# A four-layer decoder on one core: the expert layer on all eight experts, or on the two chosen per token through rows sorted in DRAM

## The chip, the cores and the metric

The kernel runs on one core of one Trainium2 chip. The metric is the device time of one execution in microseconds. The engines are PE (matmul), DVE and ACT (elementwise), POOL (GpSimd) and SP, which here only issues transfers.

## The reference, cut to what matters

x is 4 batches of 1024 tokens of 256 features, float32. Four residual layers follow one another: an attention both ways with a context of 77 rows, an expert layer, a one-head attention to the context, and an MLP with ternary weights. The expert layer is what the change touches:

```python
probs = softmax(layernorm(x) @ Wr)             # 8 experts
topk_p, topk_i = top_k(probs, 2)
# for each of the token's two experts e:  y_e = (xn @ Wi[e]) @ Wo[e]
x = x + tanh(g_ffn[0]) * sum_k(topk_p[k] * y_{topk_i[k]})
```

## The kernel before, in words

Every engine has its own program, written out by hand in the order of its work, and the programs meet at semaphores; there is no planner. An engine runs its list strictly in order. x stays in SBUF as 32 tiles of 128 tokens (x_residual), eight tiles a batch (JT), four tiles a group (G), eight groups (NG).

Stage A is the first attention, one batch after another (c = 1 to 3 in all engines' lists, batch c's scores beside a_sum of batch c-1; the a_sums of batch 3 run into stage B). Per tile, a_sum is seven products on PE, a tanh on ACT (line 1024), two updates on DVE (lines 1428, 1430) and two additions to x on POOL (lines 1778, 1780). In its first part the products Wi[e] @ Wo[e] are made and kept as wexp_h and wexp_l, a high and a low part in float32r: products of two such operands are summed as high by high, high by low and low by high.

Stage B is the expert layer, all eight experts for every token. For a group: DVE normalises (normalise, line 1276), PE transposes (line 475), ACT saves the high part and DVE the low part (lines 1098, 1526), PE makes the router logits (b_route_T, line 718), DVE chooses two (b_route, lines 1539 to 1558) and forms a weight per expert, zero for those not chosen. Then b_experts runs 16 times per group: for one tile and two experts six products of 512 columns,

```python
for k in range(KC):
    for a, c in ((xTh, wexp_h), (xTh, wexp_l), (xTl, wexp_h)):
        last = mm(ps[:, 4 + i % 4, :], a[:, s, k, j * P:(j + 1) * P],
                  c[:, k, pair * 2 * D:(pair + 1) * 2 * D], ...)
```

(line 740), and DVE adds each expert's half to x with its weight (b_add, line 1571). Work of the next group is set between these steps (b_pass, in each engine's list). In the last group's pass the second attention of group 0 (c_turn to c_attend) is set between them.

Beside stage B the weights of the MLP are loaded by SP (lines 444 to 455): ACT examines them in slices of 2048 columns, 11 in all, for low bits (examine, line 1080), rounds w1, w2, h1, w3 (line 1088), and POOL rounds h2 once the experts' weights are done with (line 1797, mlp_h_rounded). A flag says whether the weights fit the short number format; PE, ACT and DVE load it into a register (line 937 on PE) and take the short branch.

Stage D is the MLP in groups, each with the second attention of the next group set between its products (group, lines 873 to 927): w1 and w2, then h1, h2 (8 output chunks of 16 products each), then w3 with 256 columns, all on line 857. POOL adds the outcome (line 1803), SP stores it. POOL's invert makes the inverse deviation of a group's normalisation (lines 1758 and 1759, a power).

Of the kernel before, what the change touches and what calls it, by code (L numbers as in the profile page):

```python
# [27 lines left out]
F32 = mybir.dt.float32  # L28
# [14 lines left out]
G = 4  # L43
# [7 lines left out]
SLICE = 2048  # L51
REST_SLICES = (NW - HC * HID) // SLICE
# [19 lines left out]
def program(nc, d):  # L72

    ctx = ExitStack()
    with ctx:
# [42 lines left out]
        mcolb = place("small", "mask_bias_of_batch", [L, 1])  # L118
# [56 lines left out]
        E1 = place("work", "probs", [P, JT, L], at=cursor["work"] - KC * BL * 4)  # L175
        ctxr = place("work", "context", [L, B, D])
# [6 lines left out]
        c2 = place("work", "score_bias_back", [L, B])  # L183
        xn = place("work", "x_normalised", [P, JT, D])
# [10 lines left out]

        wr = place("work", "router", [P, KC, E])
        wrh = place("work", "router_high", [P, KC, E], F32R)
        wrl = place("work", "router_low", [P, KC, E], F32R)
        lgT = place("work", "logits_T", [E, GN])
        c1row = place("work", "score_bias_rows", [2, BL], at=cursor["work"] - GN * 4)  # L200
        cursor["work"] += GN * 4 - 1248
        lg = place("work", "logits", [P, G, 2 * E])
        top = place("work", "top8", [P, G, E])
        want = place("work", "to_mark", [P, G, E])
        marked = place("work", "marked", [P, G, 2 * E])
        lsub = place("work", "logits_less_max", [P, G, E])
        pex = place("work", "expert_exp", [P, G, E])
        sme = place("work", "expert_sum", [P, G])
        rie = place("work", "expert_inv", [P, G])
        rig = place("work", "expert_inv_gated", [P, G])  # L210
        pm = place("work", "expert_masked", [P, G, E])
        coef = place("work", "expert_weight", [P, 2, G, E])
        assert cursor["work"] <= wk + 4 * HC * GN * 4

        xTh = place("work", "x_T_high", [P, 2, KC, GN], F32R, at=aw_at)
        assert cursor["work"] <= dead_at
        xTl = place("work", "x_T_low", [P, 2, KC, GN], F32R, at=xt_at)
        h2_part = place("work", "mlp_h2_slice", [P, SLICE], at=dead_at)
        dump = place("work", "examined", [P, SLICE], BF16)
        assert dead_at >= aw_at + KC * GN * 8  # L220
# [19 lines left out]

        xnc = place("work", "x_norm_c", [P, G, D], at=xdh_at)
# [7 lines left out]
        mcol = place("work", "mask_bias", [L, B])  # L249

# [14 lines left out]
        rest_in = sem("mlp_rest_loaded")  # L265
# [56 lines left out]
        rt_ps = sem("router_logits_T_in_psum")  # L322
        rt_s = sem("router_logits_T_saved")
        rb_ps = sem("router_logits_in_psum")
        lg_r = sem("router_exponent_ready")
        ee_r = sem("router_exp_ready")
        y_ps = sem("expert_outputs_in_psum")
        y_free = sem("expert_bank_free")
# [18 lines left out]
        rd_r = sem("weights_slice_rounded")  # L347
        part_in = sem("mlp_h2_slice_loaded")
        h2_rd = sem("mlp_h2_slice_rounded")
# [61 lines left out]
        def pair_of(i):  # L411

            return 2 * (i // E) + i % 2, i % E // 2
# [5 lines left out]
        def _(sp):  # L419
# [20 lines left out]
            sp.wait_ge(fin, NT)  # L440
            sp.wait_ge(th_r, NT)
            sp.wait_ge(xupd, NT)

            for i, examined in enumerate((0, 1, 4, 6)):
                if i:
                    sp.wait_ge(ck_r, examined)
                rows_k = SLICE // HID
                sp.dma_start(h2_part[:].rearrange("p (k c) -> p k c", k=rows_k),
                             d["h2"][:, i * rows_k:(i + 1) * rows_k, :]).then_inc(part_in, 16)
                if i == 0:  # L450
                    for n in REST:
                        sp.dma_start(mlp_f[n], d[n]).then_inc(rest_in, 16)

            sp.wait_ge(y_ps, 4 * NT)
            sp.dma_start(mlp_f["h2"], d["h2"]).then_inc(h2_in, 16)
# [13 lines left out]
        def _(pe):  # L469
# [84 lines left out]
            def a_back_scores(c):  # L554
                pe.wait_ge(xT_r, (c + 1) * JT)
                if c == 0:
                    pe.wait_ge(map_v, 5)
                else:
                    pe.wait_ge(sf_v, 2 * c)
                for h in range(2):  # L560
# [45 lines left out]
            def a_probs_T(c):  # L606
                if c < B - 1:
                    pe.wait_ge(xT_r, (c + 2) * JT)
                for q in range(2):
# [5 lines left out]
            def a_sum(b, j):  # L615
# [23 lines left out]
                mm(ps[:, second, 0:D], IT[:, t], SSl[:, b % 2, 0:D], start=False, stop=True).then_inc(fin, 1)  # L639

# [40 lines left out]
            for c in range(1, B):  # L681
# [9 lines left out]
                a_pool(c, 1)  # L691
                a_sum(c - 1, 4)
                a_sub2char(c)
                a_sum(c - 1, 5)
                if c < B - 1:
                    a_turn(c + 1, range(0, 4))
                a_sum(c - 1, 6)
                if c < B - 1:
                    a_turn(c + 1, range(4, JT))
                a_sum(c - 1, 7)  # L700
                a_probs_T(c)
# [5 lines left out]
            def b_turn(g, s, tiles):  # L707
                for j in tiles:
# [1175 lines left out]
```

## Time and profile before

| what | value |
|---|---|
| median of 3 runs | 1144.22 us (1143.49 to 1146.84) |
| the profiled execution | 1147.13 us |
| its span, first to last instruction | 1145.2 us |
| mean granted PE clock | 0.984 of full |
| PE busy | 1094.8 us (96%) |
| DVE, ACT, POOL busy | 538.0, 449.8, 120.8 us |
| chain: PE | 84%, of it line 857 52%, line 740 13% |
| stage B, first to last expert product | 171.5 to 402.0 us |
| stage D, first product | 408.3 us |

Matmuls are pipelined: a product of 512 columns is shown as some 390 ns long while the next one starts after some 230 ns. So busy times of PE are read against the spacing of starts. "Idle before" of a group is the time in which its engine waited just ahead of it, with the releaser behind the arrow.

### The profile page before, as it was taken

The page shows a single profiled execution, that of the slowest core. Times are in us where ns is not written, and L with a number is a line of the kernel's source. Part 1 is how long each engine was busy: PE and PEld are TensorE (multiplying, and loading weights), DVE is VectorE, ACT ScalarE, POOL GpSimd, SP SyncE. Part 2 cuts the span into 40 slices and gives each one's busy share as a digit, 9 for nine tenths or more (in the row PEclk, how much of TensorE's full clock was granted, in tenths as well). Part 3 has the DMA queues.
Part 4 walks back from the last instruction along what each step waited for, and adds up shares of the span by engine and source line. Part 5 has one row for each costly group of instructions (what it writes and reads, how often), then busy time and mean ns, then how long its engine had stood idle before and what let it go on. Part 6 is the DMA issues. An engine that isn't in the chain of part 4 may idle for free.

```text
span 1145.2 us, 14891 instructions
## 1 busy us (share of the span) xinstructions
PE 1094.8 (96%) x5194; PEld 865.2 (76%) x5194; DVE 538.0 (47%) x1420; ACT 449.8 (39%) x805; POOL 120.8 (11%) x164
## 2 busy tenths in 40 slices
PE   7989979899999989999999999999999999999997
PEld 5757767677777757887887787788787788788886
DVE  6567656777777672243334235136134333422411
ACT  1344431013233244445435435435434443543532
POOL 0025552200000030010010010001001001001001
PEclk9989989999999989999999999999999999999999
DMA  9200000620110030000000000000000000000000
GB/s 343 95 1 1 1 1 1 250 82 0 37 37 0 1 147 1 1 18 2 1 19 1 1 1 20 1 0 19 1 1 19 1 1 19 1 1 1 19 1 21
DMA packets 5480, 33.31 MB, mean 29 GB/s; under 512 B 1198, under 2 KB 1454, under 8 KB 3368
## 3 DMA queue, kind: packets, MB, share of 16 engines
q1 hardware_dynamic: 4584, 29.41, 6.6%
q10 hardware_dynamic: 832, 3.02, 0.7%
q8 instruction: 44, 0.72, 0.3%
q14 instruction: 20, 0.16, 0.0%
HBM read 28.23 MB, written 4.19 MB: 28 GB/s over the span
## 4 chain that ended last, share of the span: by engine, by line
PE 84%; DVE 6%; ACT 4%; issue 3%; POOL 1%; DMA 1%; DVEq 0%; SPq 0%; POOLq 0%; ACTq 0%
PE psum L857 52%; PE psum L740 13%; PE psum L763 2%; PE psum L750 1%; PE psum L475 1%; PE psum L562 1%; PE psum L538 1%; PE psum L789 1%; PE psum L771 1%; PE psum L718 1%; PE psum L576 1%; DVE x_residual L1571 1%; DMA x_residual<-in_x 1%; PE psum L592 1%; ACT L1130 1%
## 5 line engine op out<-in xcount | busy, mean ns | idle before, releaser
L857 PE MATMUL psum<-hidden_a_high,mlp_rest_rounded 128*128 128x512 f32 x512 | 207.6, 405 | 0.0
L857 PE MATMUL psum<-hidden_b_high,mlp_h_rounded 128*128 128x512 f32 x512 | 200.6, 392 | 0.0
L857 PE MATMUL psum<-hidden_a_low,mlp_rest_rounded 128*128 128x512 f32 x512 | 199.8, 390 | 0.0
L857 PE MATMUL psum<-hidden_b_low,mlp_h_rounded 128*128 128x512 f32 x512 | 199.2, 389 | 0.0
L1685 DVE TENSOR_TENSOR hidden_a_low<-hidden_a,hidden_a_high 128x512 fp32r<-128x512 f32 x128 | 92.3, 721 | 173.9 <-ACT hidden_a_high L1195 173.1
L1685 DVE TENSOR_TENSOR hidden_b_low<-hidden_b,hidden_b_high 128x512 fp32r<-128x512 f32 x64 | 44.3, 692 | 221.2 <-ACT hidden_b_high L1195 221.2
L1571 DVE SCALAR_TENSOR_TENSOR x_residual<-psum,expert_weight,x_residual 128x256 f32 (+1 forms) x256 | 107.2, 475 | 41.1 <-PE psum L740 40.3
L857 PEld LDWEIGHTS psum<-hidden_a_high,mlp_rest_rounded 128*128 128x128 f32 x512 | 96.2, 188 | 24.2 <-issue 3.6
L857 PEld LDWEIGHTS psum<-hidden_a_low,mlp_rest_rounded 128*128 128x128 f32 x512 | 96.2, 188 | 22.2 <-issue 3.3
L857 PEld LDWEIGHTS psum<-hidden_b_high,mlp_h_rounded 128*128 128x128 f32 x512 | 96.1, 188 | 19.9
L857 PEld LDWEIGHTS psum<-hidden_b_low,mlp_h_rounded 128*128 128x128 f32 x512 | 96.1, 188 | 19.9
L857 PE MATMUL psum<-x_norm_d_T_high,mlp_rest_rounded 128*128 128x512 f32 x256 | 102.5, 400 | 6.6 <-DVE x_norm_d_T_low L1679 2.5
L740 PE MATMUL psum<-expert_high,x_T_high 128*128 128x512 f32 x256 | 105.7, 413 | 2.0 <-DVE x_residual L1571 1.7
L1209 ACT ACTIVATE hidden_a<-psum,mlp_scales 128x512 f32<-128x512 f32 x64 | 44.1, 690 | 157.7 <-PE psum L857 157.7
L740 PE MATMUL psum<-expert_high,x_T_low 128*128 128x512 f32 x256 | 101.8, 398 | 0.0
L857 PE MATMUL psum<-x_norm_d_T_low,mlp_rest_rounded 128*128 128x512 f32 x256 | 101.4, 396 | 0.0
L740 PE MATMUL psum<-expert_low,x_T_high 128*128 128x512 f32 x256 | 101.2, 395 | 0.0
L1209 ACT ACTIVATE hidden_b<-psum,mlp_scales 128x512 f32<-128x512 f32 x64 | 44.1, 689 | 118.0 <-PE psum L857 117.9
L1195 ACT ACTIVATE hidden_a_high<-hidden_a 128x512 fp32r<-128x512 f32 x128 | 80.4, 628 | 4.4 <-DVE hidden_a L1699 2.4
L1758 POOL TENSOR_TENSOR ln_var_eps<-ln_mean_var,eps 128x4 f32<-128x4 f32 (+2 forms) x28 | 6.0, 215 | 706.9 <-DVE ln_mean_var L1273 706.9
L1200 ACT ACTIVATE hidden_a<-psum,mlp_scales 128x512 f32<-128x512 f32 x64 | 44.1, 690 | 89.8 <-PE psum L857 89.8
L1699 DVE SCALAR_TENSOR_TENSOR hidden_a<-psum,mlp_scales,hidden_a 128x512 f32<-128x512 f32 x64 | 48.0, 750 | 50.4 <-ACT hidden_a L1200 50.3
(214 smaller groups left out, 1635.4 us busy)
## 6 DMA issues: line engine op xcount, KB each, us to landing
x_residual<-in_x SPq DMA_DIRECT2D x4, 1024.0 KB, 23.9
mlp_h_slice<-in_h SPq DMA_DIRECT2D x4, 1024.0 KB, 4.9
mlp_rest<-in_h SPq DMA_DIRECT2D x1, 4096.0 KB, 20.2
mlp_h<-in_h SPq DMA_DIRECT2D x1, 4096.0 KB, 12.6
out<-x_residual SPq DMA_DIRECT2D x8, 512.0 KB, 2.6
mlp_rest<-in_w SPq DMA_DIRECT2D x3, 1024.0 KB, 9.1
expert_in<-in_Wi SPq DMA_DIRECT2D x1, 2048.0 KB, 16.0
expert_out<-in_Wo SPq DMA_DIRECT2D x1, 2048.0 KB, 20.5
```

Source lines behind the costliest of these rows:

```text
L475: last = pe.transpose(ps[:, slot, k * P:(k + 1) * P], src[:, k * P:(k + 1) * P], ident[:])
L538: last = mm(ps[:, (e + 2) % 4, m * D:(m + 1) * D], wi[:, k, e, m * P:(m + 1) * P], wo[:, k, e, :], start=(k == 0), stop=(k == KC - 1))
L562: last = mm(ps[0:L, 6 + h, :], A2[:, k, c * L:(c + 1) * L], xnT[:, k, h * 512:(h + 1) * 512], start=(k == 0), stop=(k == KC - 1))
L740: last = mm(ps[:, 4 + i % 4, :], a[:, s, k, j * P:(j + 1) * P], c[:, k, pair * 2 * D:(pair + 1) * 2 * D], start=(n == 0), stop=(n == 3 * K ...
L763: last = mm(ps[:, 2 + m, :], w1t[:, k, m * P:(m + 1) * P], xcT[:, k, :], start=(k == 0), stop=(k == KC - 1))
L857: last = mm(o, a, b, start=(k == 0 and i == 0), stop=(k == n_k - 1 and i == len(parts) - 1))
L1195: act.activation(part[:, c, :], full[:, c, :], ACT.Copy).then_inc(hi_r, 1)
L1200: act.activation(ha_f[:, c, :], ps[:, d_bank(c), :], ACT.Silu, scale=sc1[:, 0, c:c + 1]).then_inc(sil_r, 1)
L1209: act.activation(full[:, c, :], ps[:, 6 + c % 2, :], ACT.Gelu, scale=sc1[:, 2 + layer, c:c + 1]).then_inc(g_r, 1)
L1571: ins = dve.scalar_tensor_tensor(of(x, G * g + j), ps[:, 4 + i % 4, h * D:(h + 1) * D], coef[:, s, j, e:e + 1], of(x, G * g + j), ALU.mult ...
L1685: dve.tensor_tensor(rest[:, c, :], full[:, c, :], part[:, c, :].bitcast(F32), ALU.subtract).then_inc(lo_r, 1)
L1699: dve.scalar_tensor_tensor(ha_f[:, c, :], ps[:, d_bank(c) + 1, :], sc1[:, 1, c:c + 1], ha_f[:, c, :], ALU.mult, ALU.mult).then_inc(h_r, 1)
```

## The change

Tokens are put in rows sorted by expert, and a tile of 128 rows is multiplied by one expert alone.

- Routing by batch in place of by group: DVE normalises a batch into xm (r_norm), PE transposes it in pairs of tiles (r_turn) and makes logits in plain float32, 8 columns each (r_logits), DVE chooses two (r_max, r_mask, r_coef). PE counts with a triangle and a column of ones (r_rank), DVE turns counts into a row number for each token and choice (slot) and a list of each tile's expert (eid), in a chain of some thirty small dependent steps (r_rank, r_tiles). A batch has at most 23 tiles (EB) of rows, in 12 pairs.
- POOL scatters the normalised tokens into DRAM (slots), 16 indirect transfers of 128 rows of 1 KB a batch, which SP has filled with zeros beforehand, and later gathers the result rows (yrows) by the same row numbers, 8 transfers a group. 128 indirect transfers in all.
- The loop over 48 pairs of tiles: SP loads four tiles at a time, PE transposes a pair (s_turn), ACT and DVE save high and low parts in two places (s_high, s_low), PE makes 12 products of 256 columns with the weights' column read from a register (s_experts, s_columns), ACT saves them and stores them to DRAM (s_save). Routing of batches 2 and 3 is set between pairs.
- Additions of the gathered rows (add_rows) and the statistics: group 0 and 1 in the loop, group g in the h2 chunks of stage D's group g - 2.
- The 22 slices of 1024 columns of the MLP's weights are now loaded behind the fills and examined within stage A (8, 8 and 6 in c = 1, 2, 3). The rounding on ACT and POOL is gone: POOL's queue loads the weights with a cast (dma_start into mlp_r).

The core of the diff:

```diff
 SP:
-            sp.wait_ge(fin, NT)
-            sp.wait_ge(th_r, NT)
-            sp.wait_ge(xupd, NT)
...
+            sp.wait_ge(ex_ps, 1)
...
+            for b in range(B):
+                dst = slots[b].rearrange("(c p j) d -> p c (j d)", c=NCK, j=CHUNK)
+                sp.dma_start(dst, d["zeros"].unsqueeze(1).broadcast_to([P, NCK, CHUNK * D])).then_inc(fill_done, 16)
...
+            for c in range(B * NCK):
+                if c % NCK == 0:
+                    sp.wait_ge(sc_done[c // NCK], 16 * 2 * JT)
+                if c >= 2:
+                    sp.wait_ge(xt_ps, min(pairs_before(c - 2) + 2, c // NCK * PAIRS if c % NCK < 2 else NP))
...
+                sp.dma_start(xs[:, c % 2, 0:n, :], chunk_rows(slots, c, n)).then_inc(xs_in[c % 2], 16)
 PE:
+            def s_turn(q):
+                c, n = chunk_of(q), pair_tiles(q)
+                pe.wait_ge(xs_in[c % 2], 16 * (c // 2 + 1))
+                if q >= 2:
+                    pe.wait_ge(xsl_r, q - 1)
...
+            def s_experts(q, columns):
+                pe.wait_ge(xsl_r, q + 1)
+                if q >= 2:
+                    pe.wait_ge(ye_r, q - 1)
+                for i in range(pair_tiles(q)):
+                    v = columns[(q % PAIRS * 2 + i) % 12]
...
+                    for k in range(KC):
+                        mm(o, xsh[:, q % 2, k, t], wexp_h[:, k, bass.ds(v, D)], start=(k == 0), stop=False)
+                        mm(o, xsl[:, q % 2, k, t], wexp_h[:, k, bass.ds(v, D)], start=False, stop=False)
+                        last = mm(o, xsh[:, q % 2, k, t], wexp_l[:, k, bass.ds(v, D)], start=False, stop=(k == KC - 1))
...
+            for q in range(NP):
+                if q % PAIRS % 6 == 0:
+                    columns = s_columns(q // PAIRS, q % PAIRS // 6)
+                s_experts(q, columns)
+                if q + 2 < NP:
+                    s_turn(q + 2)
+                for b in (2, 3):
+                    at = q - (b - 2) * PAIRS
+                    if at in (0, 2, 4, 6):
+                        r_turn(b, at // 2)
+                    if at in (1, 3, 5, 7):
+                        r_logits(b, at // 2)
+                    if at == 10:
+                        r_rank(b)
 ACT:
+            def s_save(q):
...
+                if first:
+                    act.wait_ge(ye_r, q + 1)
+                    act.dma_start(chunk_rows(yrows, c, CHUNK), ys[:, c % 2]).then_inc(st_done[c % 2], 16)
 DVE:
+            for q in range(NP):
+                if q + 2 < NP:
+                    s_low(q + 2)
...
+                    if at == 8:
+                        r_copy(b)
+                        r_max(b)
+                    if at == 9:
+                        r_mask(b)
+                    if at == 10:
+                        r_coef(b)
+                    if at == 11:
+                        r_rank(b)
+                    if at == 12:
+                        r_tiles(b)
 POOL:
+                    if b == 2 and j == 5:
+                        pool.wait_ge(fill_done, 16 * B)
+                        pool.wait_ge(ix_r, 1)
+                        scatter(0, ALL[0:3])
+                    if b == 2 and j == 6:
+                        scatter(0, ALL[3:6])
...
+                if b == 2:
+                    scatter(0, ALL[6:])
...
+            pool.wait_ge(ix_r, 2)
+            scatter(1, ALL)
+            pool.wait_ge(ix_r, 3)
+            scatter(2, ALL)
...
+            gather(0, yg0)
+            pool.wait_ge(ix_r, 4)
+            scatter(3, ALL)
...
+            gather(1, yg0)
+            for n, done in (("w1", w12_in), ("w2", w12_in), ("h1", h1_in), ("w3", h1_in)):
+                pool.dma_start(mlp_r[n], d[n]).then_inc(done, 16)
```

## Rows read from the trace of the kernel before

**Rows 1.** Busy time by stage: us, then PE, PEld, DVE, ACT, POOL, clock, DMA, GB/s.
```profile
136.00:162.00 26.00, 24.39 (x154) 19.53 (x152) 16.21 (x52) 11.84 (x44) 13.02 (x20) 1.00 0.00 1
162.00:171.00 9.00, 4.90 (x14) 1.93 (x15) 5.54 (x22) 2.12 (x5) 4.96 (x6) 0.56 0.00 0
225.00:251.00 26.00, 25.50 (x114) 19.35 (x114) 19.74 (x69) 4.03 (x8) 1.23 (x2) 1.00 0.40 162
```
**Rows 2.** The chain that ended last, in order of time: start us, us, what.
```profile
225.03 1.57 PE psum L718 x6
...
226.60 4.16 PE psum L740 x18
...
251.25 1.57 PE psum L718 x6
...
394.80 1.74 PE psum L789 x8
...
408.32 5.81 PE psum L857 x16
...
439.14 3.43 PE psum L763 x8
...
526.37 0.87 PE psum L750 x8
...
530.89 3.43 PE psum L763 x8
...
558.99 1.74 PE psum L789 x8
```
**Rows 3.** PE in order of time, products of 256 columns in the last stage.
```profile
1131.12 0.28 PE L857 MATMUL psum<-mlp_rest_rounded,hidden_a_low 128*128 128x256 f32 x1
1131.24 0.28 PE L857 MATMUL psum<-mlp_rest_rounded,hidden_a_high 128*128 128x256 f32 x1
```
**Rows 4.** Line 937: the flag loaded into a register on the PE queue.
```profile
L937 PEldq TENSOR_LOAD <-weights_not_short x1: 490/490/490, 401.1 to 401.1; - x1
```
**Rows 5.** Groups of instructions, shapes apart: busy us, mean ns, idle before.
```profile
L1571 DVE SCALAR_TENSOR_TENSOR x_residual<-psum,expert_weight,x_residual 128x256 f32 x192 | 80.5, 476 | 32.2 <-PE psum L740 31.4
L1679 DVE TENSOR_TENSOR x_norm_d_T_low<-psum,x_norm_d_T_high 128x512 fp32r<-128x512 f32 x16 | 10.7, 690 | 3.4 <-ACT x_norm_d_T_high L1187 3.4
L1187 ACT ACTIVATE x_norm_d_T_high<-psum 128x512 fp32r<-128x512 f32 x16 | 9.6, 599 | 19.4 <-PE psum L750 18.9
L1797 POOL CAST mlp_h_rounded<-mlp_h 128x2048 fp32r<-128x2048 f32 x4 | 8.8, 2241 | 7.3 <-DMA mlp_h<-in_h 7.3
L1080 ACT ACTIVATE examined<-mlp_rest 128x2048 bf16<-128x2048 uint16 x7 | 13.3, 1901 | 0.1
```
**Rows 6.** The slice loads on the SP queue, and loads with us to landing.
```profile
238.47 0.33 SPq L448 DMA_DIRECT2D mlp_h_slice<-in_h  x1
...
mlp_h_slice<-in_h SPq DMA_DIRECT2D x4, 1024.0 KB, 4.9
mlp_h<-in_h SPq DMA_DIRECT2D x1, 4096.0 KB, 12.6
```
**Rows 7.** DVE in order of time: dependent small operations of the routing.
```profile
237.58 0.23 DVE L1557 TENSOR_SCALAR expert_inv_gated<-expert_inv,gates_tanh 128x4 f32<-128x4 f32 x1
237.85 0.19 DVE L1558 TENSOR_TENSOR expert_weight<-expert_masked,expert_inv_gated 128x32 f32<-128x32 f32 x1
```
**Rows 8.** POOL and DVE after the first stage, and DVE beside a POOL cast.
```profile
162.23 1.02 POOL L1759 TENSOR_TENSOR ln_rstd<-ln_var_eps,minus_half 128x4 f32<-128x4 f32 x1
...
163.14 1.36 DVE L1276 TENSOR_SCALAR x_normalised<-x_residual,ln_mean_var,ln_rstd 128x256 f32<-128x256 f32 x4
...
163.22 1.87 POOL L1778 TENSOR_TENSOR x_residual<-x_residual,update_of_char2sub 128x256 f32<-128x256 f32 x1
165.17 0.73 POOL L1780 TENSOR_TENSOR x_residual<-x_residual,update_of_sub2char 128x256 f32<-128x256 f32 x1
...
422.70 1.72 DVE L1685 TENSOR_TENSOR hidden_a_low<-hidden_a,hidden_a_high 128x512 fp32r<-128x512 f32 x1
```

More of the change, by code:

```diff
@@ L117, in program @@
         yTb = place("small", "context_projected_of_batch", [P, KC, L])
-        mcolb = place("small", "mask_bias_of_batch", [L, 1])
+        slot = place("small", "slots_of_tokens", [P, NT, 2], I32)
+        cab = place("small", "weights_of_slots", [P, NT, 2])
         wexp_h = place("weights", "expert_high", [P, KC, E * D], F32R)
@@ L183, in program @@
         c2 = place("work", "score_bias_back", [L, B])
+        xn_at = cursor["work"]
         xn = place("work", "x_normalised", [P, JT, D])
@@ L194, in program @@
         P2 = place("work", "probs_back", [L, S])
+        small_at = cursor["work"]
         wr = place("work", "router", [P, KC, E])
[L197 to L203, printed above, removed]
@@ L215, in program @@
[L215 to L220, printed above, removed]
+        lg = place("work", "logits", [P, JT, 2 * E])
+        top = place("work", "top8", [P, JT, E])
+        want = place("work", "to_mark", [P, JT, E])
@@ new lines, in s_columns @@
+            def s_columns(b, half):
+                a, e = (0, 12) if half == 0 else (12, EB)
+                pe.wait_ge(eid_r, b + 1)
+                return nc.values_load_multi_w_load_instructions(
+                    eid[0:1, b, a:e], engines=[pe.engine], min_val=0, max_val=(E - 1) * D,
+                    skip_runtime_bounds_check_because="the column is a minimum with that of the last expert")[1]
+            def s_experts(q, columns):
[4 more added lines that the diff above has]
+                    v = columns[(q % PAIRS * 2 + i) % 12]
+                    o = ps[:, 6 + q % 2, i * D:(i + 1) * D]
+                    t = slice(i * P, (i + 1) * P)
+                    for k in range(KC):
+                        mm(o, xsh[:, q % 2, k, t], wexp_h[:, k, bass.ds(v, D)], start=(k == 0), stop=False)
+                        mm(o, xsl[:, q % 2, k, t], wexp_h[:, k, bass.ds(v, D)], start=False, stop=False)
+                        last = mm(o, xsh[:, q % 2, k, t], wexp_l[:, k, bass.ds(v, D)], start=False, stop=(k == KC - 1))
+                last.then_inc(y_ps, 1)
@@ L1770, in _, with scatter, gather @@
             pool.wait_ge(zero_ready, 7)
+            def scatter(b, pairs):
+                for j, i in pairs:
+                    pool.indirect_dma_start(slots[b], bass.IndirectOffsetOnAxis(ap=slot[:, b * JT + j, i:i + 1], axis=0),
+                                            xm[b % 2][:, j, :], None).then_inc(sc_done[b], 16)
+            def gather(g, rows):
+                for j in range(G):
+                    for i in range(2):
+                        pool.indirect_dma_start(
+                            rows[:, i, j, :], None, yrows[g // 2],
+                            bass.IndirectOffsetOnAxis(ap=slot[:, G * g + j, i:i + 1], axis=0)).then_inc(yg_in, 16)
+            ALL = [(j, i) for j in range(JT) for i in range(2)]
             for b in range(B):
@@ L1794, in _ @@
-            pool.wait_ge(h2_in, 16)
-            for i in range(n_h2 // SLICE):
-                part = slice(i * SLICE, (i + 1) * SLICE)
-                pool.tensor_copy(h2_round[:, part], h2_raw[:, part]).then_inc(h2_rd, 1)
-            def add(n):
+            pool.wait_ge(y_ps, NP)
+            pool.dma_start(mlp_r["h2"], d["h2"]).then_inc(h2_in, 16)
+            for h in range(2):
+                pool.wait_ge(st_done[h], 16 * B * NCK // 2)
+            for n in range(NG):
+                if n + 2 < NG:
+                    pool.wait_ge(sb_ps, n + 2)
+                    gather(n + 2, yg)
+                if n + 1 < NG:
+                    invert(G * (n + 1), G, n + 2, stats_c, inv_c)
+                if n + 2 < NG:
+                    invert(G * (n + 2), G, STATS_A + 3 + n)
```

837 lines of the change are left out of this document (530 added, 307 removed).

## The prediction

> **What bounds the kernel now.** I read the table of stages first, then the chain that ended last, then single instructions. In the expert stage PE is busy 25.50 of 26.00 us while DVE has 19.74, ACT 4.03 and POOL 1.23 [rows 1]. The chain shows one group of four tiles every 26.22 us (from the logits product at 225.03 to that at 251.25), nearly all of it expert products at 4.16/18 = 0.231 us each [rows 2]. All eight groups issue 8 x 16 x 6 = 768 of them, 177 us. So PE's columns bound this stage, and dropping six of eight experts per token goes at what bounds it. Ahead of it it is otherwise: in the last batch of the first stage, 136 to 162 us, DVE is busy 16.21 and ACT 11.84 of 26 us [rows 1], and PE, DVE and ACT wait for one another in turn. The last stage is PE again, 91.75 us a group (439.14 to 530.89) [rows 2]. The profiled execution took 1147.13 us, 2.9 above the median of 1144.22; the sum is made against it. The part to be replaced ends with the first product of the last stage, at 408.32 us [rows 2].
>
> **The expert products.** New: 4 batches x 23 tiles x 6 = 552 products of 256 columns. A product of that shape, its weights loaded anew each time, starts every 0.12 us [rows 3]: 66 us in place of 177. PE also transposes the sorted rows, 4 x 128 columns for a pair of tiles; eight warm ones take 0.87 [rows 2], so 0.44 a pair. A pair costs PE 12 x 0.12 + 0.44 = 1.88 us. The weights' column comes from a register; the attend product reads its operand by a constant at 394.80 and by a register at 558.99 and takes 1.74 both times [rows 2], so I charge nothing for that (bound: those products are 0.22 us apart, these 0.12, so up to 0.1 us x 552 = 55 us is not excluded by it). The columns are loaded eight times; a load of one value takes 490 ns on PE's queue [rows 4]: 4 us, up to 12 x 0.49 x 8 = 47 if each of the twelve values costs that.
>
> **The loop of a pair.** From transposes to products the pair passes ACT (rounding copy, 0.60) and DVE (low part, 0.69), while ACT also saves each result (0.60) [rows 5] and every second pair issues a store (0.33, as SP's issue) [rows 6]. With double buffers: after the products of q, transposes of q+2 0.44, products of q+1 1.44, transposes of q+3 0.44 = 2.3 us until PE wants q+2; ACT's save and copy and DVE's low part, with a few tenths of handing over, take about as long, 0.33 more on odd pairs. I take 2.05 a pair: 98 us. Beside it PE has transposes and logits of batches 2 and 3 (7 us), the attention of the first group (0.9 + 3.4 + 1.7 + 0.3 + 0.7 + 1.7 = 9 us) and the loads (4): 118.
>
> DVE is in order, so whatever stands between two low parts delays PE by its length less some 1.2 us. Dependent small operations start 0.27 us apart [rows 7], some 0.25 on average. Maxima and marks of a batch, 2.8 us; mask 1; coefficients 1.2; ranks to slots, some 21 steps, 5.4; tile experts and weights 2.4. For two batches that stalls PE 2 x 7 = 14 us; gathered additions (16 at 0.476 [rows 5]), statistics and the first update some 11 more. Loop: 118 + 25 = 143 us.
>
> **Ahead of the loop.** ACT now examines 22 half-size slices (22 x (1.90/2 + 0.19) = 25 us [rows 5]) in its own order among softmax steps; about half falls into its idle time (14 of 26 us [rows 1]): 4.5 us later per batch, the first three. Batch 0 is routed there: transposes and logits with their round trips 6 us, and 12.8 us of the DVE chain above into a window where DVE idles 10 of 26 us: 6 more. 162 + 13.5 + 6 + 6 = 187. Then, up to the first low part, DVE has a_sum (6), eight normalisations (3), fourteen tiles of statistics (7), routing of batch 1 (10.4), one more normalisation: 27 us; and it waits for POOL some 6 us, since POOL issues ten scatters ahead of the updates of batch 3. The loop starts at 220.
>
> **POOL's indirect transfers** have no row at all. Lower bound 0.33 us each (SP's issue of a plain one [rows 6]), upper 2.24 (the cast of 128x2048, the longest thing POOL does [rows 5]). I take 1.02, its small table-like operation, the power [rows 8], since 128 addresses are computed work and not a stream. At 1.02, sixteen scatters are 16 us, and each batch's rows are there a few us before PE reaches its first pair (batch 1: loop start + 16 + 2 + 3.3 = 21 against 26 us). The hidden margin ends near 1.3. One thing in the trace speaks against: beside four DVE normalisations (1.36 us together) POOL's addition takes 1.87 in place of 0.73 us [rows 8], so POOL and DVE shut one another out. I add nothing for it (24 normalisations at 0.34, at most 8 us of POOL, mostly inside the margin). The Trainium skill says so much more sharply (SBUF — State Buffer, "Who interferes with whom"): a DMA issued from GpSimd waits for its descriptors while DVE runs such an operation, one of 620 ns taking 3100; the trace agrees in direction at least. By that rule scatters beside normalisations would cost 3 us, and batches 2 and 3 would come some 10 us late. The same skill (DMA: Bandwidth & Descriptors, "Specifications") gives about 1 µs to the first byte on this path, by which the sum would stay as it is.
>
> **Filling and loading.** Four fills of 3.1 MB now go down SP's queue at 48 us ahead of the slices. At the rate of the 4 MB load (4096 KB in 12.6 us, 333 GB/s [rows 6]) they end at 87, before ACT's first examination (about 95); if each byte counts twice, as read and as written, at 125. Take 4 us late, bounds 0 and 30. A slice lands about 3.3 us after its issue (4.9 for a whole one [rows 6]).
>
> **After it.** Loop end 220 + 143 + 4 = 367, and the same 6 us to the last stage: 373 against 408.3, -35. The last stage loses POOL's four casts, beside which DVE's low part took 1.72 us [rows 8] where one takes 0.69 elsewhere [rows 5]: 4 us of DVE that PE waited for, and I give back 3. The eight gathers per group (8 us of POOL), 8 additions and 4 statistics (5.5 us of DVE) lie in h2's chunks, where DVE is idle more than half of 3.65 us a chunk: nothing, if the gathers stay under some 2 us each. Total -38: 1109 for the profiled execution, 1106 for the median; with the chance of small losses on all waits I forecast 1108.
>
> **Rivals.** (1) *POOL's issue price decides, and the kernel is slower.* If an indirect transfer holds POOL 2 us, rows of batch 1 come 37 us after loop start against 26, ranks of batch 2 only after that, and so on: +11, +15, +18 for the three batches, +8 for the second gather, some +52 and 3 in the first stage: 1163. It breaks even near 1.7 us. For it: no row, and POOL's sharing above; against: 1.02 for its power. (2) *Fill holds up ACT.* Then the first examination waits up to 30 us with everything behind it: 1120 to 1135. (3) *The loop overlaps worse on PE's clock.* Clock was 0.56 in the window 162-171, where PE was busy 4.9 of 9 us [rows 1]. If gaps keep it at the 1.2 GHz level, a pair costs 3.8 us: +70, 1178. Against it: 1.00 where PE is over 90% busy, in the windows before and behind; the loop should be near 80. (4) *Better than forecast*: ACT and DVE insertions of the first stages all fall in idle time and DVE's blocks overlap PE's extra work, 1085. (5) *Register-fed products or loads cost what the bounds allow*, cancelling the gain: 1135 to 1160.
>
> **Numbers.** Chances: forecast (1095 to 1120) 0.40; better 0.13; fill or small costs, still faster (1120 to 1141) 0.15; no change 0.05; POOL slower 0.20; clock or register costs slower 0.07. A measurement of this kernel tells 0.3%, 3.4 us, from no change. Faster 0.68, same 0.05, slower 0.27. Leaving out a tenth above and below: 1078 to 1162.
>
> **What would show it.** Products of 256 columns 0.12 us apart in blocks of twelve; pairs about 2 to 2.5 us apart, with stalls behind DVE's slot arithmetic at the twelfth pair of a batch; first product of the last stage near 373. Wrong: PE waiting for DMA (slot rows) at the first pair of a batch means rival 1; ACT waiting for a slice near 95 us, rival 2; a clock of 0.5 in the loop, rival 3; products over 0.15 apart, rival 5. The last stage should keep 91.75 us a group.

## The result, and the profile after

| | time, us | against the kernel before |
|---|---|---|
| predicted | 1108 (1078 to 1162) | faster (0.68) |
| measured | 1197.38, median of 4 (1192.81 to 1201.35) | 1143.91 beside it: ratio 1.046, interval 1.0418 to 1.0502 |

The kernel is 4.6% slower, and outside the range. The profiled execution took 1198.31 us with a span of 1196.5. Its page, with the shares by engine of the chain:

```profile
PE 1042.7 (87%) x5226; PEld 853.8 (71%) x5226; DVE 502.4 (42%) x1372; ACT 484.8 (41%) x888; POOL 238.9 (20%) x293
...
PEclk9988895569587888999999999999999999999998
...
PE 76%; ACT 5%; DVE 5%; issue 5%; another core or an unknown queue 5%; DMA 3%; POOL 0%; ACTq 0%; SPq 0%; DVEq 0%; POOLq 0%
```

PE is busy 52 us less than before (1094.8), as meant, but the span grew by 51: PE's idle time grew by 103. 5% of the chain lie with "another core or an unknown queue", on a kernel that has one core. Three rows say where. They are the first expert product and the first product of the last stage, both from the chain, and the register operations ahead of the products, whose last start dates the last pair (its last product starts at 447.6):

```profile
238.34 0.58 PE psum L909
...
455.01 5.10 PE psum L1023 x12
```
```profile
L911 PEldq ALU_OP  x184: 32/32/42, 238.3 to 446.1; - x184
```

| | predicted | measured |
|---|---|---|
| loop starts | 220 | 238.3 |
| loop lasts | 143 | 209 |
| last stage starts | 373 | 455.0 |
| last stage, with the end | 734 (737 - 3) | 741.5 |

So 66 of the 89 us between the forecast and the median, three quarters, lie in the loop of pairs. The table of stages over it (us, then PE, PEld, DVE, ACT, POOL, clock, DMA, GB/s), to be read beside [rows 1]:

```profile
136.00:162.00 26.00, 23.29 (x133) 18.36 (x134) 13.63 (x39) 16.44 (x44) 7.33 (x11) 0.82 0.41 122
190.00:220.00 30.00, 21.48 (x85) 19.23 (x84) 9.03 (x36) 4.30 (x9) 21.61 (x28) 0.50 0.26 92
220.00:238.00 18.00, 8.55 (x31) 6.88 (x29) 15.99 (x77) 2.49 (x6) 7.30 (x11) 0.50 0.08 30
...
251.00:262.00 11.00, 3.13 (x12) 1.89 (x10) 0.00 (x0) 0.47 (x1) 5.84 (x7) 0.67 0.32 118
...
298.00:324.00 26.00, 4.15 (x19) 2.80 (x17) 0.00 (x0) 0.60 (x1) 18.20 (x19) 0.59 0.38 126
...
366.00:384.00 18.00, 3.39 (x18) 2.97 (x17) 1.38 (x2) 3.31 (x6) 9.64 (x11) 0.73 0.38 135
```

In three stretches of 11, 26 and 18 us PE, DVE and ACT all but stand (PE is busy 3 to 4 us of each) and POOL alone works on: these are its streams of 16, 24 and 16 indirect transfers. No DMA bound is near (share 0.32 to 0.38). PE in order of time at the start of the first:

```profile
250.89 0.28 PE L911 MATMUL psum<-expert_low,slot_rows_T_high 128*128 x1
251.01 0.28 PE L909 MATMUL psum<-expert_high,slot_rows_T_high 128*128 x1
252.28 0.28 PE L910 MATMUL psum<-expert_high,slot_rows_T_low 128*128 x1 [1.00 <-issue]
253.70 0.28 PE L911 MATMUL psum<-expert_low,slot_rows_T_high 128*128 x1 [1.14 <-issue]
255.81 0.37 PE L909 MATMUL psum<-expert_high,slot_rows_T_high 128*128 x1 [1.83 <-issue]
```

Up to 251.01 the products are 0.12 us apart, as in [rows 3]. Then, amid the twelve products of one pair, where nothing is waited for, they are 1.3 to 2.1 us apart. ACT, in order of time, beside it:

```profile
248.75 0.60 ACT L1245 ACTIVATE slot_rows_T_high<-psum 128x512 fp32r<-128x512 f32 x1 [2.24 <-PE psum L887]
261.53 0.60 ACT L1255 ACTIVATE expert_rows<-psum 128x512 f32<-128x512 f32 x1 [12.19 <-remote]
```

Its copy at 261.53 saves the third pair. In the code (s_save) it waits for the products of that pair alone, whose last one started at 247.59, and for no store, since that wait begins with the fifth pair. So ACT stands 12 us for nothing that the program names. It goes on 2.9 us behind the stream's last transfer, which POOL ends at 258.7; the third standstill ends 2.7 (ACT) to 5.3 us (PE) behind its stream too. In the second stretch it stands for 20, and behind the streams the chain has another kind of loss:

```profile
296.27 20.56 another core or an unknown queue
...
316.87 7.68 another core or an unknown queue
...
409.34 15.76 DMA slot_rows<-slots
```

At 409 the last slot rows wait behind the weights w1, w2, h1 and w3 that POOL issued at 405 to 407. Last, the two prices that I had to bound, the load of columns and the indirect transfer (ns: least, median, longest; then first and last start):

```profile
L895 PEldq TENSOR_LOAD <-tile_expert_column x8: 1055/3954/4602, 230.0 to 430.1; - x8
...
L2076 POOL DMA_INDIRECT slots<-x_norm_of_odd_batch,slots_of_tokens x32: 956/960/1036, 238.7 to 377.7; - x32
```

A transfer's price was nearly right (1.02 taken, 0.96 measured, but 1.26 from start to start, which is what POOL pays in a row of them); the load of columns was not (0.49 taken from [rows 4], 4 at the median).

### The profile page after: what moved, and what is told of

The parts are those of the page before. It is cut to its first block, busy times and chain, and to the rows that moved or that the text cites. A ratio compares the mean times of both kernels' runs of the same rounds, so it can differ in the third digit from the quotient of the medians.

```text
span 1196.5 us, 15080 instructions
## 1 busy us (share of the span) xinstructions
PE 1042.7 (87%) x5226; PEld 853.8 (71%) x5226; DVE 502.4 (42%) x1372; ACT 484.8 (41%) x888; POOL 238.9 (20%) x293
## 4 chain that ended last, share of the span: by engine, by line
PE 76%; ACT 5%; DVE 5%; issue 5%; another core or an unknown queue 5%; DMA 3%; POOL 0%; ACTq 0%; SPq 0%; DVEq 0%; POOLq 0%
PE psum L1023 51%; PE psum L755 2%; PE psum L923 2%; PE psum L909 2%; PE psum L911 1%; PE psum L910 1%; DMA slot_rows<-slots 1%; PE psum L682 1%; PE psum L931 1%; PE psum L668 1%; PE psum L887 1%; PE psum L698 1%; PE psum L642 1%; PE psum L949 1%
## 5 line engine op out<-in xcount | busy, mean ns | idle before, releaser
L1976 DVE TENSOR_TENSOR hidden_a_low<-hidden_a,hidden_a_high 128x512 fp32r<-128x512 f32 x128 | 88.0, 687 | 137.4 <-ACT hidden_a_high L1385 136.6
L909 PE MATMUL psum<-expert_high,slot_rows_T_high 128*128 x184 | 62.9, 342 | 43.7 <-issue 25.6
L2083 POOL DMA_INDIRECT expert_rows_of_group<-yrows,slots_of_tokens x48 | 47.5, 989 | 256.1 <-PE psum L937 243.3
L1849 DVE TENSOR_TENSOR slot_rows_T_low<-psum,slot_rows_T_high 128x512 fp32r<-128x512 f32 (+1 forms) x48 | 32.0, 668 | 135.0 <-ACT slot_rows_T_high L1245 118.5
L1255 ACT ACTIVATE expert_rows<-psum 128x512 f32<-128x512 f32 (+1 forms) x48 | 27.8, 580 | 125.1 <-PE psum L911 56.1
L2059 POOL TENSOR_TENSOR ln_var_eps<-ln_mean_var,eps 128x4 f32<-128x4 f32 (+1 forms) x28 | 5.8, 206 | 359.7 <-DVE ln_mean_var L1467 359.6
L909 PEld LDWEIGHTS psum<-expert_high,slot_rows_T_high 128*128 128x128 f32 x184 | 40.5, 220 | 47.4 <-issue 47.2
```

The costliest lines, as they stand in the source:

```text
L909: mm(o, xsh[:, q % 2, k, t], wexp_h[:, k, bass.ds(v, D)], start=(k == 0), stop=False)
L1255: act.activation(ys[:, c % 2, first:first + n, :].rearrange("p j c -> p (j c)"), ps[:, 6 + q % 2, 0:n * D], ACT.Copy).then_inc(ye_r, 1)
L1849: dve.tensor_tensor(xsl[:, q % 2, :, 0:n], ps[:, 4 + q % 2, :].rearrange("p (k c) -> p k c", k=KC)[:, :, 0:n], xsh[:, q % 2, :, 0:n].bitca ...
L1976: dve.tensor_tensor(rest[:, c, :], full[:, c, :], part[:, c, :].bitcast(F32), ALU.subtract).then_inc(lo_r, 1)
L2083: pool.indirect_dma_start(rows[:, i, j, :], None, yrows[g // 2], bass.IndirectOffsetOnAxis(ap=slot[:, G * g + j, i:i + 1], axis=0)).then_i ...
```

## The experiments

Theory A: beside POOL's stream the other engines get no instructions. B: completions of ACT's stores and SP's loads are held back by a stream of transfers. C: products and loads fed by registers are slow. All edits are to the changed kernel, and each ratio is against the kernel before on the same chip. The kernels ran on five chips, those of one chip all together; which one matters, as will be seen. On the first two the unedited kernel did not run, so a difference from its 1197.4 us there is one between chips.

**First chip.** Scatters of batches 1 to 3 by SP:

```diff
-            scatter(1, ALL)
...
+                if c in (1, 1 + NCK, 1 + 2 * NCK):
+                    sp.wait_ge(ix_r, b + 1)
...
+                            sp.dma_start(slots[b][at:at + P, :], xm[b % 2][:, j, :]).then_inc(sc_done[b], 16)
```

> Left out: batches 1 to 3 of tokens are written to the sorted rows in token order, by 16 plain transfers of 128 KB each from SP in place of 16 indirect ones from POOL, so most rows meet another expert; amount of data, row loads, stores and gathers are as in the changed kernel. Theory A (instruction supply): while POOL issues indirect transfers one behind another (1.26 us from start to start), the other engines run out of instructions after some 7 to 12 us; at 251 to 261 us PE starts one instruction every 0.70 us though it waits for nothing. Then with 48 of the 64 transfers of the pair loop gone from POOL the gaps of 12, 24 and 15 us at 249-261, 298-322 and 366-384 go, but for a few us beside the gather of group 0 : 1145 to 1158 us. Theory B (completions): any stream of 128 KB transfers holds back the completions of ACT's stores and SP's loads, whoever issues it: the gaps stay, 1185 to 1205 us. Theory C (register-fed products): no change, 1190 to 1200.

Measured 1164.8 us, ratio 1.0151 (1.0091 to 1.021). The three standstills are gone. Two shorter ones (10.7 and 10.2 us) are new and of another kind: PE waits for rows which SP issues late, since its chain there is 16 issues of about 0.5 us and then

```profile
289.53 4.56 DMA slot_rows<-slots
```

The gain is less than expected, and these waits are the reason that the trace names. It speaks against B: as many bytes in as many transfers of 128 KB passed without a standstill.

Pacing:

```diff
                 for j, i in pairs:
+                    if first is not None and i == 0 and first + j:
+                        pool.wait_ge(y_ps, first + j)
```

> Same transfers, all on POOL, but two are issued per pair of tiles (POOL waits for PE's count of pairs before every second one; the gather of group 0 likewise). Theory A: POOL's stream is broken every 2.5 us, the supply of instructions recovers between, and 25 to 45 us of the 50 us of gaps go: 1150 to 1172 us; if a break of some tenths of a us is too short to recover, the gaps stay though shorter, 1175 to 1195. Theory B: the same bytes and completions beside the same stores, 1185 to 1205. Theory C: no change.

Measured 1154.6 us, ratio 1.0082 (1.0063 to 1.01): 43 us less than the changed kernel, for waits alone. The loop lasts 159 us in place of 209.

Weights later:

```diff
+            pool.wait_ge(y_ps, 44)
             for n, done in (("w1", w12_in), ("w2", w12_in), ("h1", h1_in), ("w3", h1_in)):
```

> One wait is added: POOL issues the loads of w1, w2, h1 and w3 after 44 of 48 pairs in place of right behind the gather of group 1. The wait of 15.8 us for slot rows at 409 to 425 us, in which all 16 DMA engines were busy with weights, should go; w1 and w2 then land about 12 to 24 us after issue and the last stage may wait 3 to 10 us for them. 1183 to 1192 us. If that wait belonged to the indirect transfers (A or B alone), the time does not fall, 1195 to 1210, since the weights only come later.

Measured 1188.1 us, ratio 1.038 (1.0361 to 1.04), as expected: 9 us, and the wait for slot rows is gone from the chain. Part of it comes back behind the loop: the last stage's first group takes 98.7 us in place of 94.0, with a wait of 16 us for a transfer in the chain that ends at 450.6 us.

Constant columns, which leave out the choice of the expert:

```diff
-                return nc.values_load_multi_w_load_instructions(
-                    eid[0:1, b, a:e], engines=[pe.engine], ...)[1]
+                return [0] * 12
```

> All expert products take the columns of expert 0, by a constant; the eight loads of columns and the register arithmetic ahead of each product are gone from PE's program. Theory A: PE needs about a third fewer instructions in the pair loop, runs dry later, 5 to 15 us less: 1182 to 1192. Theory B: under 5 us less. Theory C (registers slow PE): the pairs become shorter by 1 us or more and the loop by 40 us, 1150 to 1160.

Measured 1181.8 us, ratio 1.0314 (1.0281 to 1.0347), 16 us less. Two stretches of the table of stages say that the standstills are as before:

```profile
252.00:264.00 12.00, 1.09 (x5) 0.60 (x6) 0.90 (x2) 2.13 (x4) 5.98 (x7) 0.57 0.27 86
...
306.00:318.00 12.00, 1.54 (x8) 1.54 (x8) 1.40 (x3) 1.79 (x3) 9.12 (x10) 0.60 0.31 104
```

So the gain lies at the edge of A's number, but it fits the column loads as well, eight of up to 4.6 us; the edit takes out both these and the register arithmetic, and does not tell them apart. The products themselves are no closer without registers (twelve take 1.4 us at full clock in both): C can hold for the loads, not for the products.

**Second chip.** Three edits together; the scatters of batch 0 spread:

```diff
+                    if b == 3 and j < 5:
+                        scatter(0, ALL[6 + 2 * j:8 + 2 * j])
...
-                if b == 2:
-                    scatter(0, ALL[6:])
```

> The paced transfers and the later weights of the two runs before together, and the last ten scatters of batch 0 set between the updates of batch 3 on POOL, two behind each of the first five. The gaps are of different places, so their gains add: 1154.6 - 9 from the weights = 1146, and DVE's wait of 12 us for POOL at 197 to 209 us shrinks to some 3: 1135 to 1142 us. If the scatters between the updates delay each update by 2.5 us and DVE waits for it each time, the last gains nothing: 1145 to 1150.

Measured 1136.8 us, ratio 0.9923 (0.9898 to 0.9947): 0.8% faster than the kernel before.

The examination on 8 values in place of 1024, beside pacing alone:

> Left out: each examination on ACT reads 8 values of its slice in place of 1024 (the loads and all waits stay). Beside the paced transfers alone (1154.6). If ACT's time is what the examinations cost the first stage, 22 x 1 us less on ACT, of which about half was on the path: 1142 to 1148. If the wait for the next slice is the cost (some 5 us ahead of the second pair of slices of each batch), little changes: 1150 to 1154.

Measured 1139.3 us, ratio 0.9955 (0.9938 to 0.9973). It was held against 1154.6 from the first chip, which proves to be no fair comparison; see below.

Twenty-four more transfers in the last stage, whose landing POOL then waits for (cut):

```diff
                     gather(n + 2, yg)
+                if n == 1:
+                    for b in (0, 1):
+                        for j, i in (ALL if b == 0 else ALL[0:8]):
+                            pool.indirect_dma_start(slots[b], bass.IndirectOffsetOnAxis(
+                                ap=slot[:, b * JT + j, i:i + 1], axis=0), x[:, 3 * JT + 4 + i, :], None).then_inc(more_in, 16)
...
```

> The changed kernel with 24 more indirect transfers on POOL in the last stage, behind the eight gathers of its second group, at 599 to 630 us: x rows to slot rows that nobody reads any more. Nothing waits for a transfer there, and the eight gathers alone stop nobody. Theory A (instruction supply): PE has got through 136 to 174 instructions of the trace from the start of each of the loop's streams until it stood; at some 9 per us here it stands after 15 to 19 us of the 41 us, for up to 20 us: 1212 to 1225 us. Theory B (completions of stores and loads are held back): PE does not stand, 1196 to 1200.

Measured 1148.9 us, ratio 1.0034 (1.0019 to 1.005). Neither theory has this: more work, and 48 us less than the unedited kernel took on the chip of the result. The loop had none of its three standstills, though its 64 transfers stream as before.

The examinations one by one, in e5's kernel:

> As e5_combined, with ACT's examinations one at a time at 7, 8 and 7 places of the three batches in place of pairs one behind another. The waits of 4.6 to 5 us for a slice at the second pair go, in three batches: 10 to 14 us below e5_combined if those waits are on the path, the same if the other engines are waited for anyway.

Measured 1138.8 us, ratio 0.9951 (0.9932 to 0.9969): nothing gained. The waits for a slice are not on the path, or others take their place.

**Third chip.** To find whether the program or the chip made e7 fast:

> The changed kernel, not edited, once more. The kernel with 24 transfers more took 1148.9 us where this one had taken 1197.4, and its pair loop had none of the three long gaps, though the same 48 transfers stream beside it. If the gaps belong to the program, or to where its instructions and data lie, this one takes 1190 to 1200 us again, with the gaps. If they belong to the chip or to the moment (the program of 24 transfers more was run with others, later), it takes 1145 to 1160 here, without them.

> The changed kernel with one indirect transfer and one semaphore more, in the second group of the last stage. By its work 1197. If a program that differs only behind the loop has no gaps in the loop (placement of the program decides): 1145 to 1160, beside 1190 to 1200 for the unedited one.

> The paced transfers once more, on the same chip as the two before. Pacing is a cause of its own if this one is at 1150 to 1157 while the unedited one is at 1190 to 1200. If the unedited one has no gaps here, pacing is worth nothing or a little less than nothing: both within 5 us.

Measured 1198.6 (1.0472; 1.0425 to 1.052), 1195.1 (1.0439; 1.0414 to 1.0463) and 1159.9 us (1.0114; 1.0091 to 1.0138). Unedited and with one more transfer the standstills are there, and pacing takes 39 us here too.

**Fourth chip.** Unedited, with the 24 transfers, the combination, and all scatters as plain transfers that POOL issues:

> The changed kernel, not edited, for comparison on the same chip as the next three. Taken 1197.4 and 1198.6 us on two chips. If it has its three long gaps wherever it runs: 1190 to 1205. If this is a chip such as the one of the 24 extra transfers and they were its doing: 1145 to 1160.

> The changed kernel with 24 transfers more in the second group of the last stage, again. It took 1148.9 us on one chip, without gaps in the pair loop, where one transfer more took 1195.1 on another, with them. If the program decides (its length moves what the loop's instructions fall on), 1145 to 1157 again while the unedited one has 1190 to 1205. If the chip decides, the two are within 20 us of one another, whichever they are, and the extra transfers cost what they cost: 0 by theory B, up to 20 us by theory A if the gaps are there.

> Paced transfers, later weights, spread scatters of batch 0, again, beside the unedited kernel on one chip. If the gaps are there in the unedited one: 40 to 60 us below it, 1135 to 1150. If not: 10 to 20 us below it, and what pacing gives is then only an avoidance of the gaps.

> Left out: all scatters write the rows in token order, as plain transfers of 128 KB that POOL issues (same number, same bytes, same waits, no row numbers read). If a stream of POOL's transfers as such starves the others: the gaps stay, 1180 to 1200. If it is the row-wise transfer: the gaps of the scatters go and that beside the gather of group 0 stays: 1150 to 1170.

Measured 1147.9 (1.0021; 1.0005 to 1.0036), 1152.6 (1.0062; 1.0042 to 1.0083), 1135.5 (0.9922; 0.9896 to 0.9949) and 1136.5 us (0.9941; 0.9915 to 0.9966). The very same program takes 1148 us here and 1197 to 1199 elsewhere, while the kernel before keeps to 1144 to 1146 on all five chips. So it is not the program that decides but the chip, or something else that stayed the same while its kernels ran; as no chip was used a second time, no run tells these apart. "The chip" is meant so below. The table of stages of the unedited kernel on this chip:

```profile
190.00:220.00 30.00, 21.16 (x84) 19.02 (x83) 7.97 (x24) 4.30 (x9) 21.39 (x27) 0.50 0.25 92
...
251.00:262.00 11.00, 10.84 (x97) 10.76 (x95) 3.87 (x8) 5.88 (x11) 6.74 (x8) 1.00 0.93 314
262.00:291.00 29.00, 23.69 (x188) 22.90 (x187) 18.36 (x89) 12.47 (x24) 9.86 (x11) 0.94 0.64 210
298.00:324.00 26.00, 20.50 (x141) 19.67 (x141) 14.86 (x79) 10.35 (x20) 12.84 (x14) 0.83 0.65 192
```

At 251 to 262 us, amid POOL's first stream in both traces, PE is busy 10.84 of 11 us here and 3.13 there. The 24 extra transfers cost 5 us. What differs in the records is the queue named "instruction". In the second stream, on the chip of the result (296 to 322 us) and then here (280 to 306 us):

```profile
q0 software_dynamic: 998, 2.74, 31.1%
q1 hardware_dynamic: 144, 0.52, 6.8%
q10 hardware_dynamic: 144, 0.52, 6.0%
q14 instruction: 1, 0.01, 0.1%
```
```profile
q1 hardware_dynamic: 576, 1.97, 33.2%
q0 software_dynamic: 848, 2.32, 24.3%
q10 hardware_dynamic: 506, 1.88, 17.7%
q8 instruction: 2, 0.03, 0.7%
```

On the fourth chip two packets of 16 KB come over q8 within 26 us, on the chip of the result none. The Trainium skill says of such pages (Runtime: NRT & Kernel Launch, "Instruction fetch mechanics") that each sequencer fetches its next page of 256 instructions, 16 KB, over a DMA queue of its own, and that this is mostly hidden. This case agrees with the page size. That the fetch isn't hidden on some chips would be theory A, but the packets do not show it. Over the whole run both executions have 50 of them on q8, and they come at the same places of PE's work: from the one at 295.3 us to the one at 340.4 PE has 114 products in the trace of the result, from 281.9 to 298.2 it has 111 on the fourth chip; up to the next packet these are 98 and 99. So q8 goes with PE's progress, and few packets are what a PE that stands would show whatever held it. The other instruction queue, q14, has one at 301.9. From 303 to 340 us neither has any, and yet ACT went on at 316.9 and PE at 326.6: no fetch that the trace shows ended this standstill. What both traces of the unedited kernel with standstills do show is that these end 3 to 5 us behind the last transfer of POOL's stream. Theory A still fits engines that stand with nothing to wait for; it is not shown, and neither is why a chip does it.

**Fifth chip.**

> The changed kernel, not edited, once more as the measure of this chip: 1190 to 1205 us with the long gaps, or 1143 to 1152 without. It was on three chips so far, two times with and once without them.

> Paced transfers, later weights and spread scatters of batch 0. Without gaps in the unedited kernel: 12 us below it, 1130 to 1140, as on the two chips before. With them: the paced kernel alone stood at 1154.6 and 1159.9 on such chips; less 9 for the weights and up to 12 for the scatters of batch 0, 1135 to 1150: about as fast as the kernel before or a little faster, wherever it runs.

> Left out: all scatters write the rows in token order, as plain transfers of 128 KB that POOL issues. It took 1136.5 us on a chip where the unedited kernel had no gaps. If this chip has them: a stream of any transfers that POOL issues starves the others (1175 to 1195), or it is the row-wise kind alone, and only the gap beside the gather of group 0 stays (1140 to 1160).

Measured 1148.0 (1.0019; 1.0002 to 1.0035), 1135.1 (0.9912; 0.9886 to 0.9938) and 1138.4 us (0.995; 0.9926 to 0.9973). A chip without standstills once more. Plain transfers hold POOL 0.55 us in place of 0.96, and with them (they leave out the sorting, so rows meet other experts) the kernel is 11.4 and 9.6 us below the unedited one on the fourth and fifth chip. Two questions stay open: whether plain transfers from POOL would cause them, and where the combination stands on a chip that has them (the paced kernel alone stood 0.8 and 1.1% above the kernel before there).

## Why the prediction was wrong

Two misses of like size lie on one another: some 50 us appear only on some chips, and 40 would have been missed on any. For the second, the unedited kernel on the fourth chip is the measure (span 1143.4): the loop starts at 239.5 and lasts 156 us, the last stage starts at 403.8 and runs 739.6.

**What POOL's transfers do to the other engines was a term put at nothing, and it is the step that failed.** What I had for these transfers was the time that they hold POOL. On the chip of the result the other engines stood beside their streams, for 53 us in the loop (209 less 156), and pacing took back 39 us on one chip with standstills and some 43 on another. No rival had it; the nearest row [rows 8] was of POOL and DVE alone. By what mechanism they stand stays open.

Rival 1, POOL's issue price, did not come true as I put it: the price (0.96 us, start to start 1.26) lies below my break-even of 1.7, and the chain of the fourth chip has no wait for slot rows at the first pair of a batch. But the price was not free either: the cheaper plain transfers gained 10 to 11 us, on the fourth chip nearly all of it ahead of the loop, which starts at 230.9 in place of 239.5 and lasts 156 us as before. The rule that I weighed, of the Trainium skill (SBUF — State Buffer, "Who interferes with whom"), shows half a microsecond at most: the 64 scatters took 0.96 us at the median, the one at 188.0 us beside two normalisations 1.47 and others beside normalisations 0.96, nowhere near 3.1, a figure that stands in another section of that page.

**"The columns are loaded eight times ... 4 us" failed by its size.** I took the whole load of twelve values for one of [rows 4]. The eight take some 30 us together, where I had 4 and a bound of 47. On the fourth chip:

```profile
L895 PEldq TENSOR_LOAD <-tile_expert_column x8: 1052/4522/5848, 231.2 to 381.2; - x8
```

Seven of the eight stand amid the loop and cost at most 16 us in all by e4, which also drops the register arithmetic. Part of the cost is PE's clock. Behind the load at 310.2 us PE had stood for 3.6 us, the granted clock is 0.50 (314 to 318 us), and the products are 0.21 us apart:

```profile
314.95 0.57 PE L909 MATMUL psum<-expert_high,slot_rows_T_high 128*128 x1 [3.62 <-issue]
...
315.54 0.42 PE L911 MATMUL psum<-expert_low,slot_rows_T_high 128*128 x1
315.75 0.41 PE L909 MATMUL psum<-expert_high,slot_rows_T_high 128*128 x1
```

**"Loading" left out a queue.** I priced the casts that POOL lost, not the four weight loads that took their place on its queue, though every transfer that is moved was to be counted. The last slot rows wait beside them (15.76 us in the chain; 16.45 on the fourth chip); issuing them later is worth 9 us by e3.

**The loop of a pair was about right.** I took 2.05 us; pairs without routing are 1.8 to 1.9 us apart on the fourth chip, and most with it 2.3 to 2.75. Products are 0.12 apart at full clock, and constant columns make them no closer. With 16 in place of my 4 for the loads, and 9 for the weights, the sum is 143 + 12 + 9 = 164 where 156 was measured, so some 8 us of my terms were too many. The pair itself (0.2 us less, 48 times) would account for them; no run tells it from DVE's blocks between pairs.

**"The loop starts at 220" was 18 to 20 us early.** The first part held: the last low parts of the first stage (line 1611) start at 187.2 us where they started at 162.5 before, and I had 187 in place of 162. The fills were right: by the time of their landings they end at 89.5 us (87 taken), ahead of the first examination at 94.4. Two things behind 187 us failed. The ten scatters ahead of the updates of batch 3 held the chain for 12 us in place of 6:

```profile
196.79 12.22 issue
```

The fourth chip's chain names them outright, one behind another from 196.1 to 207.6 us. Spread, they give back 5 to 7 us of the loop's start (232.7 and 233.7 against 239.5 and 239.1 on two chips). These are single executions: in the ten profiled ones that share this part of the program the loop starts anywhere from 238.3 to 249.1 us. And from 190 to 239 us the granted clock is 0.50, the 1.2 GHz level. It was still mostly 1.00 in the stretch ahead of that, in which PE had little to do, during batch 0's routing on DVE and the examinations on ACT:

```profile
172.00:181.00 9.00, 3.56 (x20) 2.75 (x18) 6.83 (x35) 5.96 (x14) 1.67 (x3) 0.92 0.65 202
```

I had DVE's 27 us as the bound there and never asked for PE's. With the scatters spread the chain is PE's from 196 to 212 us, as the combination on the fifth chip shows (there POOL, busy as long, is not in it):

```profile
190.00:220.00 30.00, 25.80 (x99) 23.19 (x99) 14.88 (x64) 4.84 (x11) 26.07 (x33) 0.50 0.18 62
```

Rival 3 was this mechanism, with its weight in the wrong stage: in the loop the granted clock is 0.86 on the fourth chip. What the clock costs ahead of the loop, no run measures alone. The examination's share can't be told apart either: e6 has only kernels of other chips or edits beside it.

**The last stage** was to lose 3 us with the casts and seems to have got 3 longer (739.6 against 737). From its first to its last product it lost 1.5 (729.5 on the fourth chip against 731.0), and the groups keep their 91.7 us. The rest lies behind the last product, 10.1 us to the end against 5.9. There POOL ends its program with a wait of its own (DRAIN), first before, then changed:

```profile
L75 POOLq DRAIN  x1: 824/824/824, 1140.1 to 1140.1; - x1
```
```profile
L80 POOLq DRAIN  x1: 9100/9100/9100, 1134.1 to 1134.1; - x1
```

It grows with the transfers that POOL has issued: 7.8 us in the run that takes 48 of them away, 9.1 in the changed kernel, 9.75 with the 24 extra ones. That is 3 to 5 us at the end of every changed kernel, and the sum had no term for it. With the parts: 19.5 to the loop's start, 13 in the loop, 2 less between (8 in place of 10) and 5.6 behind it make the 36 us between 1109 and the fourth chip's profiled execution of 1145.2.

That the change doesn't pay even there (ratio 1.002 on two chips) is these 40 us. The traces name ten scatters in a row, two column loads a batch, a queue, a stretch at half clock and POOL's end; they do not price each alone. Three small edits turn it to 0.991 to 0.992 on three chips: two had no standstills, and on the third only the kernel with 24 extra transfers tells, which had none.

## What to carry to other kernels

A new kind of transfer has two prices: what it holds of its own engine, and what it does to everyone else while it streams; without a row for the second, keep it in the range, and break long streams with waits on the consumer's count. Count every load that a removed copy turns into, and look at what a path adds behind the last result. And measure a kernel that leans on a new path on more than one chip before a verdict.

## What the runs showed that was not expected

- One program takes 1197 to 1199 us on two chips or three (the first result names none) and 1148 on two others, while the kernel before stays within 0.2% on all of them. Where it is slow, PE, ACT and DVE stand beside POOL's back-to-back indirect transfers, from 4 to 12 us after the first of them until 3 to 5 us after the last.
- Eight such transfers in a row (10 us) leave PE busy in the last stage on the chips with standstills too (11.9 of 12 us from 495 us on, on the chip of the result). A stream of 32 there cost 5 us on a chip without standstills; on one with them it was not tried.
- A load of twelve values (eleven in every second one) into registers on PE's queue takes 4.5 us where one value takes 0.49. The Trainium skill gives about 200 ns per register (Runtime: NRT & Kernel Launch, "Instruction fetch mechanics"), an estimate of 2.4 us for twelve; here, from SBUF, it is nearly twice that at the median.
- POOL's end of program takes 0.8 us without transfers of its own, 7.8 to 9.8 us with 85 to 157 of them, and grows by 27 ns for each.
